# Issuing all four transfers of the shift row from GpSimd's queue

## The chip, the cores and the metric

The kernel runs on one core of a Trainium2 chip. The metric is the device time of one execution in microseconds. Engines are called by their short names in the profile: PE is TensorE, ACT is ScalarE, DVE is VectorE, POOL is GpSimd and SP is SyncE, which computes nothing here and issues transfers.

## The reference

Two batches of hidden states x (1024 tokens of 640) attend to a context of 2044 tokens (2048 less 4 appended ones) with 8 heads of width 80. A second, small attention over the 4 extra tokens is added before the output product. Cut to what matters:

```python
query = hidden_states @ Wq
keyt = enc @ Wk
valt = enc @ Wv
hs = _mha(query, keyt, valt)          # softmax(q k^T / sqrt(80)) v, 8 heads
...
out = (hs + ca_hs2) @ Wout + b_out + residual
```

All of it is float32. The kernel splits each operand into a high and a low part and adds three products.

## The kernel before, in words

The program has four stages, and each engine runs its own list of instructions, written out by hand in program order, with semaphores between engines. `project` computes queries, keys and values and stores them in scratch memory. `tokens` computes the attention over the extra tokens. `attend` is the stage of this change: 16 heads (2 batches of 8), numbered g = 0 to 15, each with 16 key tiles of 128 (t = 0 to 15; n = 16 g + t). `output` multiplies by Wout.

In `attend` PE runs, for each key tile, the scores two tiles ahead (line 1329: four matmuls of 512 columns, two with buffer `a` and two with buffer `b`), the products with the values (line 1358: six matmuls), and in between the score pieces of the next head (line 265: one matmul each, 32 for a head). ACT takes the exponential twice (lines 1268 and 1273), and DVE makes the low part (line 1201). The score pieces serve the softmax's shift. DVE reduces each piece to a maximum (line 274), and after the last piece of a head it forms the maximum of every query, negates it (lines 280 and 282) and transposes it by blocks into `mrow` (line 285, semaphore `row_done`). The result has to stand as one row of 1024 numbers in one partition of the query part of buffer `b`, where the score product adds it. Four transfers of 1 KB put it there, one for each group of 32 queries in every 128: each moves 8 rows of 32 numbers. This is "the shift".

Before the change the transfers of groups 0 and 1 are issued by SP (`shift`, line 244, semaphore `neg_in`) and those of groups 2 and 3 by GpSimd (`shift_rest`, line 253, semaphore `neg_rest`). There are two copies of the semaphores and of buffer `b`, for even and odd heads. PE waits for both counts before the first scores of a head (lines 1323 and 1324; the built program puts two of the waits into one event wait that the trace shows with line 1326).

What sets the order around them:

- The maxima of head g + 1 end in tile 11 of head g (`EARLY = 4`), and PE starts the scores of head g + 1 two tiles ahead, in its turn of tile 14 of head g. The last head has no pieces for a next one.
- SP's list in a round of head g is: wait for all scores of head g - 1, the loads of `a` for head g + 1 (line 206) and of `b` (line 218) for head g + 1, the spreading of the denominators of head g - 1 (lines 297 to 305), the load of the values (line 232), the shift of head g + 1 (line 244), and the store of head g - 1 (`put`, line 320), which waits for GpSimd's normalising. In the last rounds the loads of line 206 give way to loads of finished heads (line 1426).
- GpSimd's list in head g is: one piece of work on Wout in tile 6 (lines 1236 and 1240), four normalising pieces of head g - 1 in tiles 8 to 11 (line 313), and the shift of head g + 1 at tile 12 (line 253). For head 0 both shifts stand in `tokens` (lines 868 and 882). There, and in `project`, eight transfers of 1.5 KB (line 772) spread a similar row for the tokens.

Of the kernel before, what the change touches and what calls it, by code (L numbers as in the profile page):

```python
# [8 lines left out]
F32 = mybir.dt.float32  # L9
# [5 lines left out]
P = 128  # L15
# [12 lines left out]
ST = SQ // P  # L28
G = B * NH
# [3 lines left out]
SHIFT = D + LO_B  # L33
# [9 lines left out]
BLOCK = 32  # L43
# [44 lines left out]
class Scope:  # L88


    def __init__(self, nc, stack, sems):
        self.nc, self.stack, self.sems = nc, stack, sems
# [23 lines left out]
    def sem(self, name):  # L116
        return self.sems.enter_context(self.nc.semaphore(name))


class Heads:  # L120
# [6 lines left out]
    def __init__(self, s, spare, spare2, b1, mrow):  # L127
        sb, sem = s.sb, s.sem
        self.a = [sb(f"a{r}", [P, SKV + SQ], F32R) for r in range(2)]
        self.b = [sb("b0", [P, SKV + SQ], F32R), b1]  # L130
        s.align("v0_pad")
        self.v_s = [self.value_pair(s, 0)]
        self.one = sb("one", [P, 1])
        self.mpart = sb("mpart", [P, 2, ST, SKV // CH])
        self.mtop = sb("mtop", [P, 2, ST])
        self.mneg = sb("mneg", [P, 2, ST], F32R)
        self.mrow = mrow

        self.qk_in = [sem(f"at_qk_in{r}") for r in range(NA)]
        self.qkb_in = [sem(f"at_qkb_in{p}") for p in range(2)]  # L140
        self.neg_in = [sem(f"at_neg_in{p}") for p in range(2)]
        self.neg_rest = [sem(f"at_neg_rest{p}") for p in range(2)]
        self.v_in = [sem(f"at_v_in{p}") for p in range(2)]
        self.v_closed = sem("at_v_closed")
        self.one_done, self.kb_ones = sem("at_one"), sem("at_kb_ones")
        self.mx_full, self.mx_done = sem("at_mx_full"), sem("at_mx_done")
        self.mtop_done, self.neg_done, self.row_done = sem("at_mtop"), sem("at_neg"), sem("at_row")


        self.o_raw = [spare2[0:DA, 0:SQ], spare[0:DA, 0:SQ]]  # L150
        self.den = [None, sb("den1", [P, ST])]
        self.rden = [None, sb("rden1", [P, ST])]
        self.rbc = spare[0:D, SQ:2 * SQ]
        self.o_act = sem("at_o_act")
        self.den_in = [sem(f"at_den_in{p}") for p in range(2)]
        self.rden_done = [sem(f"at_rden{p}") for p in range(2)]
        self.rden_out, self.rbc_in, self.norm_done = sem("at_rden_out"), sem("at_rbc_in"), sem("at_norm")
        self.hs_out = [sem(f"at_hs_out{p}") for p in range(2)]

        self.s_full, self.e_done, self.ph_done = sem("at_s_full"), sem("at_exp"), sem("at_ph")  # L160
        self.pv_done = sem("at_pv")
# [73 lines left out]
    def a_loaded(self, pe, g):  # L235
        pe.wait_ge(self.qk_in[g % NA], (g // NA + 1) * 64)

    def shift(self, sp, g):

        p = g % 2  # L240
        row = self.queries_b(g)[SHIFT:SHIFT + 1, :].rearrange("o (t k q) -> o k t q", k=P // BLOCK, q=BLOCK)
        sp.wait_ge(self.row_done, g + 1)
        for k in (0, 1):
            sp.dma_start(row[:, k].bitcast(F32), self.mrow[k * BLOCK:k * BLOCK + ST, p, :]
                         ).then_inc(self.neg_in[p], 16)

    def shift_rest(self, pool, g):

        p = g % 2
        row = self.queries_b(g)[SHIFT:SHIFT + 1, :].rearrange("o (t k q) -> o k t q", k=P // BLOCK, q=BLOCK)  # L250
        pool.wait_ge(self.row_done, g + 1)
        for k in (2, 3):
            pool.dma_start(row[:, k].bitcast(F32), self.mrow[k * BLOCK:k * BLOCK + ST, p, :]
                           ).then_inc(self.neg_rest[p], 16)

    def score_piece(self, pe, mx_ps, g, k):

# [518 lines left out]
def tokens(nc, outer, kept, at, written, evicted, d, scratch):  # L776


    with ExitStack() as stack:
# [45 lines left out]
        for c in range(KC):  # L825
            q = np.flatnonzero(idx // P == c)
# [18 lines left out]
        def sync(sp):  # L845
            xv = d["x_ones"].rearrange("b (t p) (h d) -> b p t h d", p=P, d=DA)

            def values(b):
                for t in range(ST):
                    sp.dma_start(xn[b][:, t], xv[b, :, t]).then_inc(xn_in[b][t // 2], 16)  # L850

            written(sp)
            sp.dma_start(kept["wk2"][:], d["wk2_frame"]).then_inc(wk2_in, 16)
            sp.wait_ge(wk2_full, 1)
            sp.dma_start(wout[:], rows(d["wout"])).then_inc(wout_in, 16)
            at.load_a(sp, scratch, 0)
            values(0)
            sp.wait_ge(kept["ca_lo"], 1)
            sp.dma_start(onehot_f, d["onehot"]).then_inc(oh_in, 16)
            sp.wait_ge(at.kb_ones, 3)  # L860
            at.close_values(sp, scratch)
            at.load_b(sp, scratch, 0)
            sp.wait_ge(at.v_closed, 4 * 16)
            at.load_v(sp, scratch, 0)
            at.load_a(sp, scratch, 1)
            sp.wait_ge(ca0_done, NH)
            shift_tokens(sp, kept, ca[0], 0)
            at.shift(sp, 0)

        def gpsimd(pool):  # L870
            written(pool)
            for b in range(B):
                pool.memset(p2[:, b, :, 3 * (1 - b)].bitcast(F32), 0.0).then_inc(p2_zero, 1)
                pool.wait_ge(p2_zero, b + 1)
            at.fill_ones(pool, 0)
            pool.wait_ge(at.kb_ones, 3)
            pool.memset(at.one[:], 1.0).then_inc(at.one_done, 1)
            pool.wait_ge(at.one_done, 1)
            pool.wait_ge(oh_in, 16)
            pool.tensor_tensor(onehot[:], onehot_f, at.one[:].to_broadcast([P, SQ]), ALU.mult).then_inc(oh_done, 1)  # L880
            pool.wait_ge(at.kb_ones, 3)
            at.shift_rest(pool, 0)

        def scalar(act):
            def raw_out(n):
# [272 lines left out]
def attend(nc, outer, kept, at, wout, tokens_end, d, scratch):  # L1158
# [4 lines left out]
    with ExitStack() as stack:  # L1163
# [40 lines left out]
        def sync(sp, prefetch):  # L1204
            gathered(sp, B)
            sp.wait_ge(at.kb_ones, 6)
            at.load_b(sp, scratch, 1)
            at.load_a(sp, scratch, 2)
            at.load_v(sp, scratch, 1)
            sp.dma_start(wout_f, d["wout"].rearrange("(m p) n -> p m n", p=P)).then_inc(wout_in, 16)  # L1210
            at.shift(sp, 1)
            for g in range(1, G):

                sp.wait_ge(s_full, g * KT)
                if g + 2 < G:
                    at.load_a(sp, scratch, g + 2)
                else:
                    prefetch(sp, g + 2 - G)
                if g + 1 < G:
                    at.load_b(sp, scratch, g + 1)  # L1220
                at.spread(sp, scratch, g - 1)
                if g + 1 < G:
                    sp.wait_ge(pv_done, g * KT)
                    at.load_v(sp, scratch, g + 1)
                if g + 1 < G:
                    at.shift(sp, g + 1)
                at.put(sp, scratch, g - 1)

        def gpsimd(pool):
            def split_wout(k):  # L1230

                m, low = divmod(k, 2)
                hi, lo = wout
                if low:
                    pool.wait_ge(wout_hi, m + 1)
                    pool.tensor_tensor(lo[:, m, :], wout_f[:, m, :], hi[:, m, :].bitcast(F32),
                                       ALU.subtract).then_inc(wout_lo, 1)
                else:
                    pool.wait_ge(wout_in, 16)
                    pool.tensor_tensor(hi[:, m, :], wout_f[:, m, :], at.one[:].to_broadcast([P, HID]),  # L1240
                                       ALU.mult).then_inc(wout_hi, 1)

            gathered(pool, B)
            at.fill_ones(pool, 1)
            pool.wait_ge(at.kb_ones, 6)
            for n in range(N):
                g, t = divmod(n, KT)
                if n + 1 < N and on_pool[n + 1]:
                    make_low(pool, n + 1, pl_pool)
                if t == 6 and 1 <= g <= 2 * MC:  # L1250
                    wait_low(pool, n + 1)
                    split_wout(g - 1)
                if t in NORM_AT and g:
                    wait_low(pool, n + 1)
                    at.normalise(pool, g - 1, NORM_AT.index(t))
                if t == KT - EARLY and g + 1 < G:
                    at.shift_rest(pool, g + 1)
            pool.wait_ge(wout_lo, MC)

        def scalar(act):  # L1260
# [57 lines left out]
        def tensor(pe):  # L1318
            def scores(n, between):

                g, t = divmod(n, KT)
                if t == 0:
                    pe.wait_ge(at.neg_in[g % 2], (g // 2 + 1) * 32)
                    pe.wait_ge(at.neg_rest[g % 2], (g // 2 + 1) * 32)
                if n >= 2:
                    pe.wait_ge(e_done, n - 1)
                for a, y, first in ((at.keys_a(g), at.queries_a(g), True), (at.keys_b(g), at.queries_b(g), False)):
# [43 lines left out]
            for n in range(N):  # L1371
# [17 lines left out]
                while todo:  # L1389
                    between()  # L1390

        return Stage(sync, gpsimd, scalar, vector, tensor)


# [330 lines left out]
```

## Time and profile before

| | |
|---|---|
| Median of 3 runs | 1189.8 us (1189.69 to 1190.1) |
| The profiled execution | 1189.55 us |
| Its span in the profile | 1187.7 us |
| PE busy | 1180.1 us (99%) |
| DVE busy | 858.0 us (72%) |
| ACT busy | 680.5 us (57%) |
| GpSimd busy | 128.9 us (11%) |

The profile shows one execution. An engine's busy time counts its instructions, and "PEld" is PE's weight load, which overlaps its matmuls; a "q" behind an engine is its sequencer, which waits and issues transfers. Where a row of the timeline ends in brackets, it says how long the engine was idle before and who released it. The DMA time "to landing" runs from the start of the issue to the semaphore's last count.

### The profile page before, as it was taken

The numbers are of one execution on the slowest core, as the hardware profiler recorded it, in microseconds if no ns is written. First come the engines' busy times: TensorE is split into PE (matmuls) and PEld (weight loads), VectorE is DVE, ScalarE is ACT, GpSimd is POOL, SyncE is SP. The second block draws the span as 40 slices with busy tenths as digits, with TensorE's granted clock in tenths as the row PEclk, the third lists the DMA queues.
The fourth block names the chain that finished last, engine by engine and source line by source line (L and its number), as shares of the span: only waits on it lengthen the run. The fifth ranks groups of instructions, "written<-read, shape, count | busy, mean of one in ns | idle before, by whom it ended". The sixth has DMA issues, their size and how long they took to land.

```text
span 1187.7 us, 14977 instructions
## 1 busy us (share of the span) xinstructions
PE 1180.1 (99%) x5633; PEld 967.8 (81%) x5633; DVE 858.0 (72%) x1226; ACT 680.5 (57%) x797; POOL 128.9 (11%) x157
## 2 busy tenths in 40 slices
PE   9999999999999999999999999999999999999999
PEld 7888888788666678888888888888888888888998
DVE  7468624771145389989989989989899899986551
ACT  5323433222644477777777777777777777778210
POOL 1100000011000010101101110110110100110333
PEclk9999999999999999999999999999999999999999
DMA  8975785592930075264354454545436437422354
GB/s 311 356 274 178 258 311 198 218 349 96 289 74 1 1 164 137 72 152 111 92 133 111 106 118 114 117 104 135 111 90 153 109 73 167 134 60 66 101 212 142
DMA packets 140658, 178.08 MB, mean 150 GB/s; under 512 B 81241, under 2 KB 98393, under 8 KB 136746
## 3 DMA queue, kind: packets, MB, share of 16 engines
q1 hardware_dynamic: 131946, 156.30, 46.7%
q0 software_dynamic: 3888, 10.27, 2.6%
q10 hardware_dynamic: 4752, 10.55, 2.6%
q8 instruction: 44, 0.72, 0.3%
q14 instruction: 28, 0.23, 0.1%
HBM read 113.66 MB, written 63.28 MB: 149 GB/s over the span
## 4 chain that ended last, share of the span: by engine, by line
PE 95%; DVE 2%; DMA 1%; ACT 1%; issue 1%; SPq 0%; DVEq 0%; ACTq 0%
PE at_ps L1358 28%; PE bank L742 20%; PE at_ps L1329 19%; PE at_ps L265 9%; PE acc_t_ps L1107 7%; PE at_ps L1552 6%; PE s_ps L1075 2%; PE bank L719 1%; DMA x_f<-in_xT 1%; DVE prob_lo L1201 1%; PE acc_t_ps L1086 1%; PE f_ps L265 1%; PE f_ps L1028 1%; PE f_ps L1038 0%; PE at_ps L1555 0%
## 5 line engine op out<-in xcount | busy, mean ns | idle before, releaser
L274 DVE TENSOR_REDUCE mpart<-at_ps 128x1 f32<-128x512 f32 x480 | 326.2, 685 | 51.7 <-PE at_ps L265 51.1
L1268 ACT ACTIVATE prob_hi<-at_ps 128x1024 fp32r<-128x1024 f32 (+1 forms) x256 | 263.7, 1030 | 170.2 <-PE at_ps L1329 169.6
L1201 DVE TENSOR_TENSOR prob_lo<-probs,prob_hi 128x1024 fp32r<-128x1024 f32 (+1 forms) x256 | 311.5, 1217 | 19.6 <-ACT probs L1273 19.6
L1358 PE MATMUL at_ps<-prob_hi,v 128*128 128x512 f32 x1024 | 310.1, 389 | 0.0
L1273 ACT ACTIVATE probs<-at_ps 128x1024 f32<-128x1024 f32 (+1 forms) x256 | 261.5, 1021 | 0.0
L1358 PEld LDWEIGHTS at_ps<-prob_hi,v 128*128 128x128 f32 x1024 | 192.1, 188 | 40.2 <-issue 0.3
L265 PE MATMUL at_ps<-a 128*128 128x512 f32 x480 | 187.4, 391 | 0.4 <-DVE mpart L274 0.4
L1329 PE MATMUL at_ps<-a 128*128 128x512 f32 x512 | 158.1, 390 | 0.2 <-DVE vw L981 0.2
L1358 PE MATMUL at_ps<-prob_lo,v 128*128 128x512 f32 x512 | 157.8, 389 | 0.1
L1329 PE MATMUL at_ps<-b 128*128 128x512 f32 x512 | 157.7, 389 | 0.0
L1358 PEld LDWEIGHTS at_ps<-prob_lo,v 128*128 128x128 f32 x512 | 96.0, 188 | 20.5 <-DVE prob_lo L1201 0.5
L1329 PEld LDWEIGHTS at_ps<-a 128*128 128x128 f32 x512 | 96.0, 188 | 20.5 <-DVE vw L981 0.5
L1329 PEld LDWEIGHTS at_ps<-b 128*128 128x128 f32 x512 | 96.1, 188 | 19.7
L265 PEld LDWEIGHTS at_ps<-a 128*128 128x128 f32 x480 | 90.1, 188 | 21.6 <-DVE mpart L274 2.5
L570 ACT ACTIVATE out_hi<-bank 128x512 fp32r<-128x512 f32 x60 | 35.1, 597 | 104.4 <-PE bank L742 104.4
L660 DVE TENSOR_TENSOR out_lo<-bank,out_hi 128x512 fp32r<-128x512 f32 x60 | 40.2, 688 | 51.9 <-ACT out_hi L570 51.7
L742 PE MATMUL bank<-x_hi,wq_store 128*128 128x512 f32 x200 | 64.6, 394 | 0.0
L915 ACT ACTIVATE p<-s_ps 128x768 f32<-128x768 f32 x42 | 34.0, 810 | 49.1 <-PE s_ps L1075 49.1
L742 PE MATMUL bank<-wv_hi,ctx_hi 128*128 128x320 f32 x192 | 60.0, 313 | 0.7 <-DVE out_lo L660 0.7
L642 DVE TENSOR_REDUCE pj_part<-bank 128x1 f32<-128x512 f32 x96 | 59.4, 680 | 0.0
L742 PE MATMUL bank<-wv_hi,ctx_lo 128*128 128x320 f32 x192 | 59.3, 309 | 0.0
L742 PE MATMUL bank<-wv_lo,ctx_hi 128*128 128x320 f32 x192 | 59.3, 309 | 0.0
(154 smaller groups left out, 1354.6 us busy)
## 6 DMA issues: line engine op xcount, KB each, us to landing
v_hi_d<-v_t SPq DMA_DIRECT2D x16, 648.0 KB, 6.4
v_lo_d<-v_t SPq DMA_DIRECT2D x16, 648.0 KB, 8.4
v<-v_hi_d SPq DMA_DIRECT2D x16, 648.0 KB, 6.0
v<-v_lo_d SPq DMA_DIRECT2D x16, 648.0 KB, 7.8
k_hi_d<-out_hi SPq DMA_DIRECT2D x40, 256.0 KB, 5.1
k_lo_d<-out_lo SPq DMA_DIRECT2D x40, 256.0 KB, 6.2
a<-k_hi_d SPq DMA_DIRECT2D x16, 640.0 KB, 7.3
b<-k_hi_d SPq DMA_DIRECT2D x16, 640.0 KB, 11.1
```

What stands on the lines that cost most here:

```text
L265: pe.matmul(to, self.queries_a(g)[:, qt * P:(qt + 1) * P], self.keys_a(g)[:, c * CH:(c + 1) * CH], start=True, stop=True).then_inc(self.mx ...
L274: dve.tensor_reduce(self.mpart[:, g % 2, qt, c:c + 1], at[:, 0:w], AX, ALU.max).then_inc(self.mx_done, 1)
L642: dve.tensor_reduce(part[:, h * KC + kc, u:u + 1], bank[:], AX, ALU.max).then_inc(done, 1)
L660: dve.tensor_tensor(lo[:], bank[:], hi[:].bitcast(F32), ALU.subtract).then_inc(done, 1)
L742: mm = pe.matmul(to, a, y, start=k == 0 and i == 0, stop=k == nk - 1 and i == 2)
L1107: mm = pe.matmul(acc_ps[n % 2], xn[b][:, 2 * j + t, h, :], p1[k % 3][:, t, :], start=j == 0 and t == 0, stop=j == pairs - 1 and t == 1)
L1201: eng.tensor_tensor(pl[n % PL][0:r, :], prob[n % PF][0:r, :], ph[n % PB][0:r, :].bitcast(F32), ALU.subtract).then_inc(sem, 1)
L1268: act.activation(ph[n % PB][0:r, :], s_ps[n % 2][0:r, :], ACT.Exp, scale=SCALE).then_inc(ph_done, 1)
L1273: act.activation(prob[n % PF][0:r, :], s_ps[n % 2][0:r, :], ACT.Exp, scale=SCALE).then_inc(e_done, 1)
L1329: mm = pe.matmul(s_ps[n % 2][:, u * CH:(u + 1) * CH], a[:, t * P:(t + 1) * P], y[:, u * CH:(u + 1) * CH], start=first, stop=not first)
L1358: mm = pe.matmul(wide[3][:, u], a[:, t, :], y[:, u * CH:(u + 1) * CH], start=t == 0 and m == 0, stop=t == KT - 1 and m == 2)
L1552: pe.matmul(ps[:, u, 0:cuts[u + 1] - cuts[u]], a[:, m, tokens_of], y[:, m, cuts[u]:cuts[u + 1]], start=m == 0 and k == 0, stop=False)
```

## The change

`shift_rest` is gone. `shift` now issues all four transfers and is called on GpSimd alone, where `shift_rest` was called. SP's three calls are removed. All four count the one semaphore `neg_in`, and PE waits for 64 in place of two waits for 32.

```diff
-    def shift(self, sp, g):
-
-        p = g % 2
-        row = self.queries_b(g)[SHIFT:SHIFT + 1, :].rearrange("o (t k q) -> o k t q", k=P // BLOCK, q=BLOCK)
-        sp.wait_ge(self.row_done, g + 1)
-        for k in (0, 1):
-            sp.dma_start(row[:, k].bitcast(F32), self.mrow[k * BLOCK:k * BLOCK + ST, p, :]
-                         ).then_inc(self.neg_in[p], 16)
-
-    def shift_rest(self, pool, g):
+    def shift(self, pool, g):
 
         p = g % 2
         row = self.queries_b(g)[SHIFT:SHIFT + 1, :].rearrange("o (t k q) -> o k t q", k=P // BLOCK, q=BLOCK)
         pool.wait_ge(self.row_done, g + 1)
-        for k in (2, 3):
+        for k in range(P // BLOCK):
             pool.dma_start(row[:, k].bitcast(F32), self.mrow[k * BLOCK:k * BLOCK + ST, p, :]
-                           ).then_inc(self.neg_rest[p], 16)
+                           ).then_inc(self.neg_in[p], 16)
...
             shift_tokens(sp, kept, ca[0], 0)
-            at.shift(sp, 0)
...
             pool.wait_ge(at.kb_ones, 3)
-            at.shift_rest(pool, 0)
+            at.shift(pool, 0)
...
             sp.dma_start(wout_f, d["wout"].rearrange("(m p) n -> p m n", p=P)).then_inc(wout_in, 16)
-            at.shift(sp, 1)
...
-                if g + 1 < G:
-                    at.shift(sp, g + 1)
                 at.put(sp, scratch, g - 1)
...
                 if t == KT - EARLY and g + 1 < G:
-                    at.shift_rest(pool, g + 1)
+                    at.shift(pool, g + 1)
...
                 if t == 0:
-                    pe.wait_ge(at.neg_in[g % 2], (g // 2 + 1) * 32)
-                    pe.wait_ge(at.neg_rest[g % 2], (g // 2 + 1) * 32)
+                    pe.wait_ge(at.neg_in[g % 2], (g // 2 + 1) * 64)
```

SP's list in the first round of `attend`, before: the denominators of head 0, the values of head 2, the shift of head 2 (`b<-mrow`), and the store of head 0 (`heads_d`).

```order
L305 DMA x_f<-rden_d 80x1024 [waits at_rden_out]
L232 DMA v<-v_hi_d 128x16x81 [waits at_pv]
L232 DMA v<-v_lo_d 128x16x81
L244 DMA b<-mrow 1x8x32 [waits at_row]
L244 DMA b<-mrow 1x8x32
L320 DMA heads_d<-x_hi_place 80x1024 [waits at_norm]
L206 DMA a<-q_hi_d 80x1024 [waits at_s_full]
```

The same place in the changed kernel (its lines are numbered 1 to 15 lower):

```order
L295 DMA x_f<-rden_d 80x1024 [waits at_rden_out]
L231 DMA v<-v_hi_d 128x16x81 [waits at_pv]
L231 DMA v<-v_lo_d 128x16x81
L310 DMA heads_d<-x_hi_place 80x1024 [waits at_norm]
L205 DMA a<-q_hi_d 80x1024 [waits at_s_full]
```

The two transfers and SP's wait for the row are gone, and the store of the finished head follows the loads of the values.

GpSimd's list in head 1, before: the work on Wout, four normalising pieces of head 0, and its two transfers of head 2's shift.

```order
L1240 TENSOR_TENSOR wq_store<-ca_f,one 128x640 [waits at_wout_in,at_pl_dve]
L313 TENSOR_TENSOR x_hi_place<-x_hi_place,x_f 80x256 [waits at_rbc_in,at_pl_dve]
L313 TENSOR_TENSOR x_hi_place<-x_hi_place,x_f 80x256 [waits at_rbc_in,at_pl_dve,at_norm] x3
L253 DMA b<-mrow 1x8x32 [waits at_row,at_norm]
L253 DMA b<-mrow 1x8x32
L1236 TENSOR_TENSOR wq_store<-ca_f,wq_store 128x640 [waits at_wout_hi,at_pl_dve]
```

In the changed kernel:

```order
L1226 TENSOR_TENSOR wq_store<-ca_f,one 128x640 [waits at_wout_in,at_pl_dve]
L303 TENSOR_TENSOR x_hi_place<-x_hi_place,x_f 80x256 [waits at_rbc_in,at_pl_dve]
L303 TENSOR_TENSOR x_hi_place<-x_hi_place,x_f 80x256 [waits at_rbc_in,at_pl_dve,at_norm] x3
L243 DMA b<-mrow 1x8x32 [waits at_row,at_norm]
L243 DMA b<-mrow 1x8x32 x3
L1222 TENSOR_TENSOR wq_store<-ca_f,wq_store 128x640 [waits at_wout_hi,at_pl_dve]
```

Four transfers now stand in a row where two stood, behind the same waits.

## Rows read from the trace of the kernel before

**Rows 1.** The page: shares of the engines, and the chain that ended last.
```profile
PE 1180.1 (99%) x5633; PEld 967.8 (81%) x5633; DVE 858.0 (72%) x1226; ACT 680.5 (57%) x797; POOL 128.9 (11%) x157
...
PE 95%; DVE 2%; DMA 1%; ACT 1%; issue 1%; SPq 0%; DVEq 0%; ACTq 0%
```

**Rows 2.** Stretches: us, busy PE, PEld, DVE, ACT, POOL, then clock, DMA share, GB/s.
```profile
462.00:1066.00 604.00, 604.00 (x2665) 499.81 (x2664) 544.93 (x720) 444.77 (x472) 68.61 (x92) 1.00 0.49 115
1066.00:1110.00 44.00, 43.92 (x194) 35.75 (x193) 33.34 (x40) 36.15 (x39) 4.35 (x7) 1.00 0.17 54
```

**Rows 3.** Timeline around head 2's shift: start, length, engine, line, out<-in, idle before.
```profile
499.21 0.74 POOL L313 TENSOR_TENSOR x_hi_place<-x_hi_place,x_f 80x256 f32<-80x256 f32 x1 [1.98 <-DVE prob_lo L1201]
...
500.14 0.21 DVE L285 STREAM_TRANSPOSE mrow<-mneg 128x32 f32<-128x32 f32 x1
...
500.38 1.41 SPq L244 DMA_DIRECT2D b<-mrow  x2
...
500.90 1.04 POOL L253 DMA_DIRECT2D b<-mrow  x2 [0.95 <-DVE mrow L285]
...
501.84 0.43 SPq L320 DMA_DIRECT2D heads_d<-x_hi_place  x1
...
503.14 0.78 SPq L206 DMA_DIRECT2D a<-q_hi_d  x2
...
504.31 0.41 PEld L1329 LDWEIGHTS at_ps<-a 128*128 128x128 f32 x2
```

**Rows 4.** Timeline around head 14's shift.
```profile
1023.52 1.04 POOL L253 DMA_DIRECT2D b<-mrow  x2 [0.95 <-DVE mrow L285]
...
1026.93 0.41 PEld L1329 LDWEIGHTS at_ps<-a 128*128 128x128 f32 x2
```

**Rows 5.** Timeline around head 0's shift.
```profile
396.96 1.08 POOL L253 DMA_DIRECT2D b<-mrow  x2 [75.45 <-DVE mrow L285]
...
415.15 0.19 PEld L1329 LDWEIGHTS at_ps<-a 128*128 128x128 f32 x1
```

**Rows 6.** Timeline around head 1's shift.
```profile
457.57 1.00 POOL L253 DMA_DIRECT2D b<-mrow  x2 [33.88 <-DVE mrow L285]
...
460.76 0.41 PEld L1329 LDWEIGHTS at_ps<-a 128*128 128x128 f32 x2
```

**Rows 7.** Timeline around head 15's shift.
```profile
1067.04 1.03 POOL L253 DMA_DIRECT2D b<-mrow  x2 [0.96 <-DVE mrow L285]
...
1068.60 0.39 SPq L1426 DMA_DIRECT2D b<-heads_d  x1
...
1069.54 0.41 PEld L1329 LDWEIGHTS at_ps<-a 128*128 128x128 f32 x2
```

**Rows 8.** GpSimd's small transfers, and DMA issues with KB and us to landing.
```profile
L253 POOL DMA_DIRECT2D b<-mrow x32: 497/512/573, 397.0 to 1067.6; - x32
...
DMA to landing us min/median/max: 1.5/1.6/1.9
...
260.08 4.30 POOL L772 DMA_DIRECT2D ca<-ntop  x8 [115.25 <-DVE ntop L597]
...
heads_d<-x_hi_place SPq DMA_DIRECT2D x8, 320.0 KB, 2.8
...
ca<-ntop POOLq DMA_DIRECT2D x8, 1.5 KB, 4.0
```

**Rows 9.** PE's event wait of line 1326 ahead of heads 1 and 2: ns, then start.
```profile
L1326 PEldq EVENT_SEMAPHORE  x1: 432/432/432, 459.4 to 459.4; - x1
...
L1326 PEldq EVENT_SEMAPHORE  x1: 338/338/338, 502.7 to 502.7; - x1
```

**Rows 10.** Stretches with the DMA engines' share: the last columns are PEclk, DMA share, GB/s.
```profile
260.00:264.00 4.00, 4.00 (x25) 3.65 (x24) 1.63 (x4) 1.64 (x3) 3.92 (x8) 1.00 1.03 381
1069.50:1071.00 1.50, 1.50 (x8) 1.23 (x8) 0.46 (x2) 1.18 (x3) 0.00 (x0) 1.00 0.91 194
```

**Rows 11.** Timeline of DVE in the last head.
```profile
1089.05 1.23 DVE L1201 TENSOR_TENSOR prob_lo<-probs,prob_hi 128x1024 fp32r<-128x1024 f32 x1 [1.04 <-ACT probs L1273]
```

More of the change, by code:

```diff
@@ L141, in __init__ @@
         self.neg_in = [sem(f"at_neg_in{p}") for p in range(2)]
-        self.neg_rest = [sem(f"at_neg_rest{p}") for p in range(2)]
         self.v_in = [sem(f"at_v_in{p}") for p in range(2)]
```

## The prediction, made before the changed kernel was run

> **What bounds the kernel now.** I read four views in this order: the page's shares, the chain that ended last, the stretches of the attention stage, and then the timeline around each head's shift. The first says that TensorE (PE) works in 99% of the span, and the chain is 95% PE and 1% DMA [rows 1]. The stretches say it more sharply: from 462 to 1066 us PE is busy 604.00 of 604 us at a granted clock of 1.00, and from 1066 to 1110 us it is idle for 0.08 us in all [rows 2]. So no microsecond of the attention stage is spent waiting for the shift's transfers, and taking work off the loading queue (SP) gives PE nothing back. The change can only be neutral or cost something. The question is whether the row of maxima still reaches buffer b before PE asks for it, once it goes through one queue instead of two.
>
> **What the row has to meet.** In a middle head the order is: VectorE's transpose writes mrow, the two queues issue two transfers each, and PE loads the first key tile of the new head with the first load of line 1329. For head 2 these stand at 500.14 + 0.21 = 500.35 us, 500.38 (SP), 500.90 (GpSimd) and 504.31 us [rows 3]. What matters is the time from GpSimd's first issue to PE's load, because the issue and the landing have to fit into it. It is 3.41 us in head 2 and in head 14 [rows 3, 4], and the heads between repeat the pattern every 43.55 us. Head 0 has 18.19 us [rows 5], head 1 3.19 us [rows 6]. Head 15 has the least, 1069.54 - 1067.04 = 2.50 us [rows 7]: the last two tiles before it carry no score pieces for a next head, so PE comes to it sooner.
>
> **A recipe for the landing, tried on what is known.** GpSimd issues two transfers in 1.04 us and, for the token rows, eight in 4.30 us, which is 0.52 to 0.54 us each; I take 0.53. From issue to landing its mrow transfers take 1.5 / 1.6 / 1.9 us (least, median, most) [rows 8]. Head 2's second transfer should then land at 500.90 + 0.53 + 1.6 = 503.03 us. PE's sequencer, which runs ahead of its engine, stood in the wait of line 1326 from 502.7 for 0.338 us, to 503.04 us [rows 9]. The recipe fits, and the same row shows that this wait costs nothing: the engine still had queued work until 504.31 us.
>
> **The change, part by part.** *Removed from SP:* 32 issues, 1.41 us per head [rows 3], and 16 waits for the row. Behind them on SP stood the store of the finished head (line 320) and then the next loads. The store waits for GpSimd's last normalising piece, which ends at 499.21 + 0.74 = 499.95 us, so it goes out near 500.0 instead of 501.84 us. The loads of line 206 wait for PE's scores and were issued 0.9 us after SP was free, so they stay at 503.14 us [rows 3]. Nobody on PE's road waits for the store. Worth: 0. *Added to GpSimd:* 32 issues, 2 x 0.53 = 1.06 us per head. What stands behind them on GpSimd is the next head's work in its seventh tile, many tiles later, so the occupation costs 0. *The merged semaphore:* PE now waits for one count of 64 in place of two of 32; the event wait is hidden as above, worth 0.
>
> *The landing of the fourth transfer* is the one term that counts. It is issued 3 x 0.53 = 1.59 us after the first and lands 1.6 us later, so 3.19 us are needed from GpSimd's first issue on.
> - Head 0: 18.19 us are there: no cost [rows 5].
> - Head 1: 457.57 + 3.19 = 460.76 us, the very time of PE's load [rows 6]. PE's wait there ended at 459.4 + 0.43 = 459.8 us, where the recipe gives 459.7 [rows 9], so this head runs some 0.1 us late: **+0.1 us**.
> - Heads 2 to 14: 3.41 us are there. The landing comes at 504.09 us against 504.31, and at 1026.71 against 1026.93, a margin of 0.22 us, thirteen times: **0**.
> - Head 15: 1067.04 + 3.19 = 1070.23 us against 1069.54 [rows 7]: **+0.7 us**. SP issues a load of 1280 KB at 1068.60, and the DMA engines' share is 0.91 after 1069.5 us [rows 10], while the fourth transfer is in flight. Its price lies between 0 and 2.4 us: the token rows, issued while the engines were full (share 1.03), landed 4.0 us after issue instead of 1.6 [rows 8, 10]. The load has only begun by then, so I take a value near the low end: **+0.1 us**.
>
> A late start is passed on in full: PE works in order. VectorE still waits 1.04 us for ScalarE at 1089.05 us, just before it becomes the busier engine in the last tiles [rows 11], so it starts those later too. The sum is 0.1 + 0.7 + 0.1 = 0.9 us on the profiled execution's 1189.55 us (span 1187.7), which gives 1190.45. The median of the runs is 0.25 us above that execution, so I forecast 1189.8 + 0.9 = **1190.7 us**. The low end of the sum, with landings of 1.5 us, is 0.6; with landings of 1.9 us everywhere it is 0.08 x 13 + 0.4 + 1.0 = 2.4 us, and up to 4.8 us with the full price of the collision.
>
> **Where a rule speaks against the change.** In the rows, a GpSimd transfer of 1 KB lands 1.6 us after its issue, and the margin of 0.22 us rests on that [rows 8]. The Trainium skill (DMA: Bandwidth & Descriptors, section on the anatomy of one DMA on the GpSimd path) gives such a DMA a fixed cost of about 2.0 us. By that rule the fourth transfer would be 0.18 us late in each of 13 heads, and the kernel would take about 1193.6 us. The trace does not agree with it here (1.6 us measured), so the sum goes by the row.
>
> **Rivals.** *First, the other side: the fourth landing slips past the margin in every head (slower).* The place is the first load of line 1329 in heads 2 to 14, and the deciding point is a landing of 504.31 - 502.49 = 1.82 us after issue. At 2.1 us the price is 0.28 x 13 = 3.6 us, plus 0.6 in head 1 and 1.2 in head 15: 5.4 us, or 1195.2 us. For it: four transfers now follow each other in one queue; the highest landing of before, 1.9 us, is already beyond the point; and the store of 320 KB, freed from SP's wait, lands 2.8 us after its new issue near 500.0 [rows 8] and so lies over the first transfers. Against it: by 502.49 us the store is nearly through, the loads issued at 503.14 come after, and half of the 32 landings were at or under 1.6 us. The same mechanism in a mild form (1.95 us) gives 1193.0 us. The rule above is this rival too.
>
> *Second, head 15's lateness is not seen in the end:* the last tiles are bound by VectorE, and part of the 0.7 us goes into waits of other engines. That gives about 1190.0 us. Against it stands VectorE's wait of 1.04 us [rows 11].
>
> *Third, faster:* the early store or the quieter SP queue would have to shorten a wait of PE, and there is only 0.08 us of idle time after 462 us to take [rows 2]. 1189.7 us at best, unless something outside these rows moves.
>
> *That the change does not do what it says* I exclude: the built order shows the four issues together on GpSimd and none on SP.
>
> **How the numbers follow.** The forecast gets 0.70, the second rival 0.08, the first 0.19 and a gain 0.03. A difference within 0.2% (2.4 us, about what a measurement of this kernel can tell from no change) holds the forecast and the second rival: 0.78. Slower by more than that is the first rival: 0.19. Faster: 0.03. The range runs from 1189.7 (no cost, less the spread of the runs) to 1193.5 us, which takes in the landings of 1.9 us in all heads and the milder half of the first rival.
>
> **What would show it.** In the changed profile, GpSimd's groups at the shift should be four issues in about 2.1 us, starting 0.55 us after the transpose as before, and the store of line 320 should start near 500.0 us in head 2. PE's event wait before the first scores should be about 1.4 us long, ending 0.2 us before the load, with the load still 3.41 us after GpSimd's first issue in heads 2 to 14. In head 15 that distance should grow from 2.50 us by 0.7 to 0.9. I am wrong if PE shows idle time before that load in the middle heads, if the issues take longer than 0.56 us when four follow each other, or if landings lie above 1.8 us.

## The result, and the profile after

The changed kernel takes **1193.11 us** (median of 8 runs, 1192.69 to 1194.97) against 1189.65 us of the kernel before (8 runs, 1189.55 to 1190.1): a ratio of 1.0033 with a 95% interval of 1.0024 to 1.0042. That is 3.5 us more, or 0.3%, and so slower by more than 0.2%. The profiled execution took 1194.97 us, with a span of 1192.9 us: 5.4 us more than the profiled execution before, and the slowest of the eight. So its profile shows 1.9 us more than the median has.

The middle heads first, in the timeline of the changed kernel (start, us, engine, line, operation; the numbers of lines are 1 to 15 lower than before). These rows answer to [rows 3]:

```profile
500.16 0.31 SPq L310 DMA_DIRECT2D heads_d<-x_hi_place  x1
500.32 0.21 DVE L275 STREAM_TRANSPOSE mrow<-mneg 128x32 f32<-128x32 f32 x1
...
501.09 2.04 POOL L243 DMA_DIRECT2D b<-mrow  x4 [0.96 <-DVE mrow L275]
...
503.32 0.78 SPq L205 DMA_DIRECT2D a<-q_hi_d  x2
...
504.49 0.41 PEld L1314 LDWEIGHTS at_ps<-a 128*128 128x128 f32 x2
```

Four issues take 2.04 us, the store goes out at 500.16 us, and PE's weight load that needs the row comes 504.49 - 501.09 = 3.40 us after the first issue, without a bracket: PE did not wait. Before it was 3.41 us. One announced sign is not to be seen: the event wait before the first scores, now at line 1311, lasts 51 ns in all 16 heads, so where PE's sequencer stands for the row can't be read from it.

Now the stretches of the attention stage, with head 15's start cut out (columns: stretch, its length, then for each engine busy time and instructions, granted clock, DMA share, GB/s). The first row answers to [rows 2], and the other four cover what was one row there:

```profile
462.00:1066.00 604.00, 604.00 (x2663) 499.47 (x2663) 544.77 (x719) 444.54 (x472) 81.16 (x118) 1.00 0.48 115
1066.00:1069.90 3.90, 3.90 (x19) 3.24 (x18) 3.08 (x6) 3.02 (x4) 2.54 (x5) 1.00 0.30 85
1069.90:1072.40 2.50, 0.46 (x3) 0.04 (x1) 1.30 (x2) 1.08 (x2) 0.00 (x0) 1.00 0.88 236
1072.40:1076.00 3.60, 3.52 (x8) 2.80 (x9) 0.00 (x0) 1.40 (x2) 0.00 (x0) 0.53 0.52 200
1076.00:1110.00 34.00, 34.00 (x150) 27.80 (x149) 25.01 (x28) 28.95 (x32) 3.23 (x4) 1.00 0.07 20
```

Up to 1066 us PE is listed as busy throughout. That does not exclude a short wait, for the ends of matmuls are modelled: some 0.4 us are lost in head 14 inside this row, as the timeline below shows. After 1069.9 us PE works 0.46 of 2.50 us, and right behind that the granted clock is 0.53 over 3.60 us: the lower of the clock's two levels, 1.2 of 2.4 GHz, for nearly all of it. Heads 14 and 15 in the timeline, which answer to [rows 4, 7]:

```profile
1023.64 2.04 POOL L243 DMA_DIRECT2D b<-mrow  x4 [0.95 <-DVE mrow L275]
...
1025.88 0.39 SPq L1411 DMA_DIRECT2D a<-heads_d  x1
...
1027.41 0.30 PEld L1314 LDWEIGHTS at_ps<-a 128*128 128x128 f32 x2 [0.41 <-DMA b<-mrow]
...
1067.47 2.03 POOL L243 DMA_DIRECT2D b<-mrow  x4 [0.95 <-DVE mrow L275]
...
1069.03 0.39 SPq L1411 DMA_DIRECT2D b<-heads_d  x1
...
1072.48 0.50 PEld L1314 LDWEIGHTS at_ps<-a 128*128 128x128 f32 x2 [2.55 <-DMA b<-mrow]
1072.48 1.22 PE L1314 MATMUL at_ps<-a 128*128 128x512 f32 x2 [2.12 <-DMA b<-mrow]
```

In head 14 PE's load comes 3.77 us after GpSimd's first issue where it was 3.41 us, and in head 15 5.01 us where it was 2.50 us. SP's load of 1280 KB goes out at 1069.03 us, within 0.03 us of the fourth issue. The transfers of head 15 as a group, in the view of the tile `mrow` from 1066 to 1073 us, put a number on the landing:

```profile
L243 POOL DMA_DIRECT2D b<-mrow x4: 499/506/545, 1067.5 to 1069.0; - x4
...
DMA to landing us min/median/max: 1.5/1.7/3.4
```

The 3.4 us are those of the fourth: it went out at 1069.0 us, and PE's load starts at 1072.48 us. The last part of the loss is behind PE's work. The view of the program's last line shows GpSimd's final drain, the instruction with which its list ends (columns: least, median and most ns, then start); first before, then after:

```profile
L1637 POOLq DRAIN  x1: 5861/5861/5861, 1179.8 to 1179.8; - x1
```

```profile
L1622 POOLq DRAIN  x1: 8474/8474/8474, 1184.2 to 1184.2; - x1
...
1190.20 0.36 SPq L1460 DMA_DIRECT2D out<-probs  x1
```

The last store is issued at 1190.20 us (1185.78 us before) and lands 1.5 us later in both. Before, the drain was over at 1185.7 us, and the span ended 1.9 us after that issue. Now it ends at 1192.7 us, and the span 2.7 us after the issue.

So the 5.4 us of this execution are: about 0.4 in head 14, 2.5 in head 15 (5.01 - 2.50), and 1.5 behind it, where the clock was low (the last store is issued 4.4 us later, less those two). The drain adds 0.8 us, which makes the 5.2 us by which the span grew; the rest, 0.2 us, lies outside the span. The low clock does not come in every execution: the five of 1192.7 to 1193.1 us had a mean clock of 1.000, the three of 1194.3 to 1195.0 us had 0.998.

### The profile page after: what moved, and what is told of

It reads as the page before. It is cut to its first block, busy times and chain, and to the rows that moved or that the text cites. A ratio compares the mean times of both kernels' runs of the same rounds, so it can differ in the third digit from the quotient of the medians.

```text
span 1192.9 us, 14977 instructions
## 1 busy us (share of the span) xinstructions
PE 1183.1 (99%) x5633; PEld 969.5 (81%) x5633; DVE 854.8 (72%) x1226; ACT 680.8 (57%) x797; POOL 144.6 (12%) x189
## 4 chain that ended last, share of the span: by engine, by line
PE 96%; DVE 2%; issue 1%; ACT 0%; DMA 0%; POOL 0%; DVEq 0%; POOLq 0%; ACTq 0%
PE at_ps L1343 28%; PE bank L732 20%; PE at_ps L1314 19%; PE at_ps L255 9%; PE acc_t_ps L1096 7%; PE at_ps L1537 6%; PE s_ps L1064 2%; PE bank L709 1%; DVE prob_lo L1190 1%; PE bank L678 1%; PE acc_t_ps L1075 1%; PE f_ps L255 1%; PE f_ps L1017 1%; PE f_ps L1027 0%; PE at_ps L1540 0%
```

## The experiments

**The loads held back.** The changed kernel, in which SP waits in the last two rounds for the shift of the head, before it issues the loads of finished heads:

```diff
                 else:
+                    sp.wait_ge(at.neg_in[g % 2], (g // 2 + 1) * 64)
                     prefetch(sp, g + 2 - G)
```

> All four transfers stay on GpSimd, but SP waits for the landing of head 15's (and head 14's) shift before it issues the load of a finished head (1280 KB). Collision theory (that load's traffic holds up the fourth transfer): the fourth lands 1.5 to 1.6 us after its issue in heads 14 and 15, the stall before head 15 shrinks from 2.5 to about 0.6 us, no stretch at the lower clock, time 1190.1 to 1190.5. Queue theory (four in a row from GpSimd are slow to finish by themselves): the fourth of head 15 still takes over 3 us, time about 1193.

Measured: 1190.93 us (1190.52 to 1192.24, 10 runs), ratio 1.0012 [1.0002, 1.0021] to 1189.64 us. Its timeline in head 15:

```profile
1067.27 2.02 POOL L243 DMA_DIRECT2D b<-mrow  x4 [0.95 <-DVE mrow L275]
...
1070.34 0.30 PEld L1315 LDWEIGHTS at_ps<-a 128*128 128x128 f32 x2 [0.60 <-DMA b<-mrow]
...
1070.36 0.39 SPq L1412 DMA_DIRECT2D b<-heads_d  x1
```

With the load held back, the fourth lands 1.5 us after its issue, PE's load comes 3.07 us after the first issue, and the idle time is 0.60 us: the lateness that I had priced at 0.7. The clock stays at 1.00. The time is still 0.4 us above what I expected. The drain explains it: here it takes 8476 ns, as long as in the changed kernel. The experiment with the drain by itself prices it at 0.7 us.

**Only head 15 split, and only head 15 together.** The one run keeps head 15's first two transfers on SP and puts all others on GpSimd, the other has the split of before in heads 0 to 14 and puts head 15's four on GpSimd. SP's transfers count a semaphore of their own; `on_sp(g)` says how many it issues (in the second run `0 if g == G - 1 else 2`):

```diff
+    def on_sp(g):
+        return 2 if g == G - 1 else 0
...
-        for k in range(P // BLOCK):
+        for k in range(self.on_sp(g), P // BLOCK):
```

> The change everywhere but in head 15, whose shift is split again (two transfers on SP, two on GpSimd). If nearly the whole loss sits in head 15: 1189.8 to 1190.3, with 0.3 us left in head 14. If the loss were spread over the heads: 1192 or more.

> The reverse of the run before: split as before in heads 0 to 14, all four on GpSimd in head 15 alone. If the whole loss sits in head 15: 1192.5 to 1194.8, as the full change, with the fourth transfer landing over 3 us after its issue. If it were spread: within 0.5 us of 1189.7.

Measured: 1190.2 us (1190.03 to 1191.7), ratio 1.0007 [0.9997, 1.0016], with head 15 split; 1193.49 us (1191.73 to 1193.91), ratio 1.0026 [1.0015, 1.0037], with head 15 alone on GpSimd. In the first no head waits, not even head 14, though its four transfers are all on GpSimd and SP's load of 1280 KB goes out 0.7 us after the fourth (issued near 1025.3 us), just as in the changed kernel. The timeline, and the landings of its last two transfers:

```profile
1023.76 2.03 POOL L263 DMA_DIRECT2D b<-mrow  x4 [0.95 <-DVE mrow L295]
...
1026.00 0.39 SPq L1438 DMA_DIRECT2D a<-heads_d  x1
```

```profile
L263 POOL DMA_DIRECT2D b<-mrow x2: 497/502/508, 1024.8 to 1025.3; - x2
DMA to landing us min/median/max: 1.5/1.5/1.5
```

In the profile of the changed kernel the four of head 14 landed 1.9, 1.9, 1.9 and 2.2 us after their issues, the first three of them issued more than 1 us before that load. So head 14's wait is not shown to come from the load, and it need not come in every execution.

In the second run head 15 waits:

```profile
1067.25 2.02 POOL L263 DMA_DIRECT2D b<-mrow  x4 [0.95 <-DVE mrow L295]
...
1068.81 0.39 SPq L1438 DMA_DIRECT2D b<-heads_d  x1
...
1072.07 0.30 PEld L1341 LDWEIGHTS at_ps<-a 128*128 128x128 f32 x2 [2.36 <-DMA b<-mrow]
```

One head of sixteen carries the loss, but for the drain (6017 ns here, as good as before): moving two transfers of 1 KB in it costs 2.1 to 2.3 us (three runs of 1191.7 to 1192.0 us at a mean clock of 1.000) or 4 us (four of 1193.5 to 1193.9 at 0.999).

**Three on GpSimd and one on SP,** in all heads (`on_sp` is 1):

> In every head GpSimd issues three transfers and SP one. The last GpSimd issue comes 0.5 us earlier than with four, ahead of SP's load of 1280 KB in head 15. Collision theory: its last transfer lands 1.5 to 1.6 us after issue, at about the time PE needs it, time 1189.7 to 1190.2. If the cost grew with each issue that is moved to GpSimd, half of the loss: 1191.3.

Measured: 1191.86 us (1191.16 to 1198.19, 10 runs), ratio 1.0025 [1.0015, 1.0034]. My expectation missed, and this taught the most. SP's store of 320 KB (line 330) now goes out between GpSimd's transfers. Head 2 in the timeline, and its transfers as a group:

```profile
501.16 1.53 POOL L263 DMA_DIRECT2D b<-mrow  x3 [0.95 <-DVE mrow L295]
501.39 0.43 SPq L330 DMA_DIRECT2D heads_d<-x_hi_place  x1
```

```profile
DMA to landing us min/median/max: 1.6/2.4/2.5
```

The store holds the small transfers up as well, by 0.9 us: in most middle heads they just reach PE in time. In heads 12, 14 and 15 of the profiled execution they don't, and the last of the three lands 4.5, 4.6 and 3.8 us after its issue. The view of `mrow` over the whole span says:

```profile
  PEld at_ps L1341: 6.9, 3
...
DMA to landing us min/median/max: 1.5/2.4/4.6
```

This is the slowest of the ten executions (1198.19 us); six of them took 1191.2 to 1192.1 us and can't have had all three waits. Head 12 has the same issues in the same order as the middle heads that don't wait, and no run shows what sets it apart.

**The same with SP held until GpSimd's three have landed:**

```diff
+                if g + 1 < G:
+                    sp.wait_ge(at.neg_in[(g + 1) % 2], at.counts(g + 1)[1])
                 at.put(sp, scratch, g - 1)
```

> The three-and-one split of the run with three transfers on GpSimd and one on SP, with one wait more: in every round SP waits until GpSimd's three have landed before it issues the store of the finished head, and so everything behind it. If SP's traffic is what holds GpSimd's landings: the third lands 1.5 to 1.6 us after its issue in every head, no head stalls PE, and the time is 1189.6 to 1190.0 us (67 transfers make a drain of 7.2 us, which is still hidden). If the length of GpSimd's queue is what slows a landing, the wait changes nothing: landings up to 2.4 us, stalls in heads 12, 14 and 15 as before it, 1191.3 us or more.

Measured: 1189.62 us (1189.47 to 1190.05, 11 runs) beside 1189.6 us, ratio 1.0 [0.9992, 1.0009]. Nobody is listed as waiting for `b` any more, and the landings are back:

```profile
L263 POOL DMA_DIRECT2D b<-mrow x48: 497/508/572, 397.1 to 1068.0; - x48
...
DMA to landing us min/median/max: 1.5/1.5/1.9
```

One wait of SP takes away all that three transfers on GpSimd had cost. So for three transfers it is not the length of GpSimd's queue, but what SP's queue moves meanwhile.

**The drain by itself.** The kernel before with its shift as it was, and 32 tiny transfers more on GpSimd (8 numbers each, to a spare place), four each in the third tile of heads 0 to 7:

```diff
+                if t == 2 and g < 8:
+                    at.extra(pool, scratch["spare"], g, 4)
```

> The kernel before with its shift untouched, and 32 more tiny transfers (8 rows of one number to a spare place in memory) on GpSimd's queue, four each in the third tile of heads 0 to 7, where GpSimd is idle: 83 of its transfers in all, as in the changed kernel. If GpSimd's final drain grows with the number of transfers that it has issued: 8.4 to 8.5 us in place of 5.9, its end 2.6 to 2.7 us after the issue of the last store in place of 1.95, no stall of PE anywhere, and 1190.3 to 1190.5 us. Rival, the drain's length comes from what the shift itself does (which copies, when): it stays near 5.9 us, and the time at 1189.6 to 1189.8 us.

Measured: 1190.28 us (1190.17 to 1190.44, 11 runs) beside 1189.6 us (1189.46 to 1189.86): the two sets do not overlap, though the ratio's interval (1.0006 [0.9997, 1.0014]) is wider than their difference of 0.7 us. The drain, before 5861 ns:

```profile
L1646 POOLq DRAIN  x1: 8472/8472/8472, 1179.8 to 1179.8; - x1
```

Nothing else moved: the last store is issued at 1185.85 us, 0.07 us later than before. The drain is as long as in the changed kernel (8474 ns), after the same number of transfers, 83, though the last of the extra ones went out over 400 us before the end. Over all runs it was 5861 ns for 51 transfers, 6017 for 53, 7176 for 67, 7497 for 71, 8314 for 81, 8474 for 83, 8714 for 86 and 8974 for 89: some 0.08 us for each.

**Both costs taken away.** The loads held back as in the first experiment, and heads 0 to 5 split again (`on_sp` is 2 for them), which leaves 71 transfers on GpSimd:

> The changed kernel with the loads held back in the last two rounds, and with heads 0 to 5 split over both queues as before: 71 transfers on GpSimd. If the collision and the drain are the whole of the change's cost, this takes both away: a drain of 7.4 to 7.6 us that ends at or before SP's last landing, no stall in any head, and 1189.8 to 1190.4 us. If the drain is not what cost the last 0.7 us in the run with the held loads, it stays at 1190.8 to 1191.0 us.

Measured: 1190.19 us (1190.01 to 1190.66, 11 runs), ratio 1.0005 [0.9996, 1.0014]. The drain takes 7497 ns and is over before the last store has landed. What is left over 1189.6 us is head 15's own lateness: the view of `mrow` lists one wait.

```profile
  PEld at_ps L1342: 0.6, 1
```

**A stall in the middle of the stage.** The kernel of the first experiment, with six transfers of 1 KB to a spare place ahead of head 8's shift, once with SP's loads of that round where they were and once held back:

```diff
+        for k in range(extra):
+            pool.dma_start(spare[k:k + 1, :].rearrange("o (t q) -> (o t) q", t=ST), self.mrow[0:ST, p, :]
+                           ).then_inc(self.extra_out, 16)
```
```diff
                 sp.wait_ge(s_full, g * KT)
+                if g == 8:
+                    sp.wait_ge(at.neg_in[0], (g // 2 + 1) * 64)
```

> The changed kernel with the loads held back in the last two rounds (1190.9 us), and six transfers of 1 KB to a spare place in memory on GpSimd's queue ahead of head 8's shift, 0.5 us each: the fourth landing of head 8 comes some 3.1 us later, 2.6 to 2.9 us after PE wants it. Theory: the stall is passed on in full, and the clock that PE is granted falls to 0.5 for 3.4 us behind it, worth 1.5 us more; with 0.5 us of longer drain that gives 1195.2 to 1195.9 us, the clock's part perhaps only in some executions (then 1193.8 to 1194.4 for those without). Rival: in the middle of the stage such a stall is made good, or the clock's fall belongs to the end of the stage alone: 1191.4 to 1194.4 us in all executions, with the clock at 1.00.

> The same with six transfers ahead, the loads of head 8's round held back: the one difference to the run that stalled 10.1 us. Theory, the loads were the whole of the excess: landings 1.5 us after issue, a stall of 2.5 to 2.8 us, and 1193.9 to 1194.3 us where the clock stays at 1.00; where it falls to 0.5 behind the stall, 1.5 us more (1195.3 to 1195.9 us), as in the changed kernel's head 15, whose stall was a little shorter. Rival, GpSimd's queue of ten transfers slows its own landings: a stall well over 3 us, and 1197 us or more.

> A stall in the middle of the stage without a collision: the changed kernel with the loads held back in the last two rounds and also in head 8's round until the fourth transfer has landed, and three transfers of 1 KB to a spare place ahead of head 8's shift (0.5 us each). Theory: the fourth landing of head 8 comes 1.5 us after its issue, PE stalls 1.0 to 1.3 us there, the clock stays at 1.00, and the time is that of the held loads (1190.9 us) plus the stall plus 0.24 us of drain: 1192.1 to 1192.5 us in all executions. Rival, a late landing costs far more than its lateness even without the loads beside it (as the stall of 10.1 us in the run with six would have it): landings over 3 us and 1194 us or more.

Measured: 1203.09 us (1202.64 to 1204.2, 4 runs), ratio 1.0115 [1.0101, 1.0128], with the loads where they were. Held back, 1195.77 us (1193.93 to 1196.88, 4 runs), ratio 1.0045 [1.0029, 1.0062]. With three extra transfers in place of six, held back, 1192.69 us (1192.42 to 1194.47, 8 runs), ratio 1.0029 [1.0019, 1.0039]. The first missed my figure by 7 us, and its timeline tells why:

```profile
764.45 0.96 SPq L206 DMA_DIRECT2D a<-q_hi_d  x2
765.20 1.98 POOL L247 DMA_DIRECT2D b<-mrow  x4
765.47 0.41 SPq L206 DMA_DIRECT2D a<-k_hi_d  x1
...
769.17 0.49 SPq L218 DMA_DIRECT2D b<-k_lo_d  x1
...
775.69 0.50 PEld L1320 LDWEIGHTS at_ps<-a 128*128 128x128 f32 x2 [10.11 <-DMA b<-mrow]
```

The four transfers went out together with the loads of the next two heads (`a` for head 10 and `b` for head 9: the kernel loads `a` two heads ahead, not one as the section on the kernel before has it), and PE stood still for 10.11 us. The landings of the last two:

```profile
L247 POOL DMA_DIRECT2D b<-mrow x2: 497/502/508, 766.2 to 766.7; - x2
DMA to landing us min/median/max: 6.1/7.5/9.0
```

With the loads held back everything else is the same, and the stall is 2.67 us:

```profile
765.22 1.98 POOL L247 DMA_DIRECT2D b<-mrow  x4
768.27 0.30 PEld L1322 LDWEIGHTS at_ps<-a 128*128 128x128 f32 x2 [2.67 <-DMA b<-mrow]
```

The difference, 7.4 us, is the price of the loads alone, and the medians differ by 7.3 us. The clean run also shows the clock, in its stretches around that stall:

```profile
765.60:769.00 3.40, 1.15 (x5) 0.63 (x4) 0.84 (x2) 0.81 (x1) 1.60 (x4) 1.00 0.02 2
769.10:772.40 3.30, 3.30 (x9) 2.61 (x8) 2.51 (x3) 1.94 (x2) 0.00 (x0) 0.50 0.85 211
772.50:800.00 27.50, 27.50 (x122) 22.72 (x121) 23.73 (x31) 19.82 (x22) 1.56 (x1) 1.00 0.65 143
```

Behind PE's idle time the clock is 0.50 for 3.3 us, though PE is busy in all of them, and then 1.00 again. In the run with three extra transfers PE's load waited 1.24 us and the clock stayed at 1.00:

```profile
766.00:768.00 2.00, 1.18 (x5) 0.67 (x4) 0.83 (x2) 0.80 (x1) 0.14 (x1) 1.00 0.02 1
```

A stall in head 8 is passed on in full, as one in head 15 is: 1190.93 + 1.24 + 0.24 of longer drain makes 1192.4 us, and five of the eight runs with three lay at 1192.4 to 1192.8 us. The other three took 1193.9 to 1194.5 us, which my expectation of 1192.1 to 1192.5 us in all executions did not have; their mean clock was 0.999 to 1.000, and no profile shows what they lost. The clean run with six expected 1193.9 to 1194.3 us without the fall of the clock and 1.5 us more with it; its four executions took 1193.93, 1195.59, 1195.95 and 1196.88 us, the last of them the profiled one. Their mean clocks, 0.999, 0.998, 0.998 and 0.999, do not tell which of the other three had the fall.

## Why the prediction was wrong

I predicted 1190.7 us, 0.9 us more than before, with 0.78 on "within 0.2%"; the kernel came out 3.5 us slower than before. The range, 1189.7 to 1193.5 us, holds the median of 1193.11 us, but not the three executions with the low clock.

- **What bounds the kernel, and no gain:** right. But "no microsecond of the attention stage is spent waiting", read from PE's busy time, is finer than that row can tell: after the change it says 604.00 of 604 us again, with head 14's wait inside it.
- **The recipe for the landing:** right. Four issues take 2.04 us where about 2.1 stood, and the fourth lands 1.5 us after its issue in heads 2 to 13 (1.6 in head 12), which therefore cost nothing. The rule of the Trainium skill that I had set against it, a fixed cost of about 2.0 us for a small GpSimd transfer (DMA: Bandwidth & Descriptors, the anatomy of one DMA on the GpSimd path), would have made the middle heads late; the trace, with 1.5 us, does not agree with it here.
- **Head 1, +0.1 us:** no wait is seen there; the landing of 1.5 us took the margin back.
- **Head 15's lateness, +0.7 us:** right, 0.60 us once nothing else is in the way.
- **Head 15's collision, +0.1 us:** this is the step that failed. "The load has only begun by then, so I take a value near the low end" was a wish. The fourth transfer landed 3.4 us after its issue in place of 1.5, and head 15 grew by 2.5 us, of which 0.6 is lateness: the term was 1.9 us. With the load held back it was nothing. My upper bound for it, 2.4 us, held, but it came from a stretch in which the engines had long been full; the run with six extra transfers shows that it was no bound (9.0 us).
- **Head 14, 0:** PE waits 0.41 us there in the profiled execution, with a fourth landing of 2.2 us. Why stays open: the load of `a<-heads_d` goes out 0.7 us after the fourth issue, but with the same spacing the fourth landed after 1.5 us in the run with head 15 split.
- **The low clock, not in the sum:** the lateness and the collision together make an idle time of 2.1 us on PE, and behind it the clock fell in some of the executions, for 1.5 us more.
- **The end of the program, not in the sum:** I had costed 32 added issues on GpSimd at 0, because nothing waits behind them. The drain stands behind them, and 32 more transfers make it longer: 0.7 us, shown by itself.
- **The first rival** had the right sign and the wrong place. It asked for lateness in thirteen heads; it was one head, at the point where two things that I priced separately meet. Its idea that the freed store lies over the first transfers is seen: the first landing of head 2 went from 1.5 to 1.9 us. With the store held back, as in the quiet run of three and one, it is 1.6 us. It costs nothing there, since the fourth counts.
- **The second rival** did not come: none of head 15's lateness was made good behind it.
- **The sum as it should have been:** 0.6 + 1.9 (head 15) + 0.7 (drain) = 3.2 us without the clock's part, and 3.6 us where head 14 waits 0.4 us too. The five executions with the high clock lay 3.0 to 3.5 us above the median before.

## What to carry to other kernels

A small transfer on GpSimd's queue can land late when the loading queue moves much beside it: look at what else is issued shortly before it and until it has landed, and do not price a coincidence near 0 because it has only begun. When the last of several transfers is moved later, as here by a second pair ahead of it, check the head with the least margin for what it is moved into. Where such a transfer feeds the busiest engine, one wait that holds the large transfers back until it has landed can remove the whole of it, as it did here with three and one (1189.62 us).

## What the runs showed of the hardware

- **Small transfers beside large ones.** A GpSimd transfer of 1 KB landed 1.5 us after its issue alone, 1.9 us behind a store of 320 KB that went out 0.9 us earlier, 2.4 us beside one that went out between the small ones, 3.4 us beside a load of 1280 KB, and up to 9.0 us beside the loads of two heads. A load that goes out 0.7 us behind it need not hold it up (1.5 us in head 14, with head 15 split). In the run with six and the loads in place the four landed 3.7, 5.4, 6.1 and 9.0 us after issues 0.5 us apart, that is 2.2, 1.2 and 3.4 us after one another. By the Trainium skill (DMA: Bandwidth & Descriptors, Queues, rings and completion order) a DMA engine takes turns between its queues and finishes a whole packet of one, some 9 to 17 descriptors, before it turns to the next. These distances would fit one turn for each small transfer, but no run varied the packets, so this mechanism stays argued.
- **The final drain of GpSimd** lasted 0.08 us more for each transfer that it had issued, whenever that was, and set the end of the program from some number between 71 and 81 on: with 71 the span ended 1.95 us after the last store's issue, as before (1.9), with 81 2.2 us, with 83 2.7 us.
- **The clock** fell to 0.50 behind idle times of PE of 2.1 and 2.3 us (the brackets at its matmuls), and in the idle time of 9.7 us it fell before PE began again (0.50 from 768.9 to 775.6 us). It did not fall behind 0.8 us, nor behind 1.8 us in heads 12 and 14 with three and one. Behind 1.93 us, with head 15 alone on GpSimd, it stayed at 1.00 in the profiled execution, and behind 1.95 us, with three and one, it fell. The same kernel had it in some executions and not in others.
- **Open:** in the profiled execution of the clean run with six, head 14's fourth transfer landed 3.5 us after its issue, while the DMA engines' share was 0.03 and SP issued nothing. PE's load waited 1.7 us for it. It was seen once, and no run here explains it; the executions of that run spread over 3 us. So not every late landing is a collision with SP's traffic, and one profiled execution alone would not have proved it for head 15: the medians with and without the load's wait do.
